# Fewer and wider small products in a decoder kernel: scores by masked keys, queries and scaled keys in one product, and half of a solve's last product

## What is computed

```python
# block 1, delta rule, 4 heads of 32: q and k have length 1
pred = einsum('bhk,bhkv->bhv', k_t, S); err = (v_t - pred) * b_t
S = S + einsum('bhk,bhv->bhkv', k_t, err); o_t = einsum('bhk,bhkv->bhv', q_t, S)
# block 2, attention over ctx, 16 heads of 8, causal
scores = einsum('bhqd,bhkd->bhqk', qh, kh) / sqrt(8); attn = softmax(causal(scores))
# block 4, self attention, 16 heads of 8, q and k of length 1
scores = clip(einsum('bhqd,bhkd->bhqk', q, k) * 0.25, -5, 5); softmax(causal(scores) / 1.5)
# block 5, gated attention over ctx, 8 heads of 16
C = einsum('bhid,bhjd->bhij', qh, kh) * exp(Dtilde - max_d) / 4
```

## Time and profile before

| | |
|---|---|
| median of three runs | 4670.56 us |
| profiled execution, its own time | 4663.74 us |
| its span | 4662.0 us |
| TensorE busy | 4477.5 us, 96% of the span |
| VectorE, ScalarE, GpSimd busy | 3554.0, 3497.4, 2654.2 us |
| instructions of TensorE | 66736 matmuls and as many loads |
| chain of waits that ended last | PE 91%, DVE 4%, ACT 3% |

### The profile page before, as it was taken

One profiled execution on the slowest core, in us unless ns is written; L12 is line 12 of the kernel. 1 busy time (PEld: TensorE's weight loads), 2 busy tenths in 40 slices (PEclk: granted clock), 3 DMA queues, 4 the chain that ended last, 5 costly groups with the idle time before them and its releaser, 6 DMA issues.

```text
span 4662.0 us, 160117 instructions
## 1 busy us (share of the span) xinstructions
PE 4477.5 (96%) x66736; PEld 3503.7 (75%) x66736; DVE 3554.0 (76%) x11069; ACT 3497.4 (75%) x9695; POOL 2654.2 (57%) x2212
## 2 busy tenths in 40 slices
PE   7999989999999999999999999999999879999999
PEld 5777767777777777777777777777777668888888
DVE  4555568988888888888888888888888546776675
ACT  3444458888888888888888888888888547776676
POOL 3344357777667666667766667766677423333332
PEclk8777779999999999999999999999999869999999
DMA  3000000000000000000000000000000100000000
GB/s 97 4 4 4 4 2 2 2 2 2 25 2 2 2 2 25 2 2 2 25 2 2 2 25 2 2 2 2 9 6 6 44 1 4 4 4 4 4 4 6
DMA packets 40236, 40.83 MB, mean 9 GB/s; under 512 B 4164, under 2 KB 37976, under 8 KB 38744
## 3 DMA queue, kind: packets, MB, share of 16 engines
q1 hardware_dynamic: 39512, 30.59, 2.2%
HBM read 28.48 MB, written 2.10 MB: 7 GB/s over the span
## 4 chain that ended last, share of the span: by engine, by line
PE 91%; DVE 4%; ACT 3%; issue 1%; POOL 1%; SPq 0%; DMA 0%; ACTq 0%; DVEq 0%; POOLq 0%
PE ps L532 75%; PE ps L536 16%; ACT BIG L883 2%; DVE BIG L1085 1%; ACT L883 1%; DVE sm L1096 1%; DVE BIG L1093 1%; DVE BIG L1090 0%; POOL BIG L1521 0%; DVE sm L1093 0%; ACT BIG L875 0%; POOL sm L1524 0%; DVE sm L1085 0%; DVE BIG L1163 0%; DVE sm L1191 0%
## 5 line engine op out<-in xcount | busy, mean ns | idle before, releaser
L875 ACT ACTIVATE BIG<-ps 128x512 f32<-128x512 f32 (+6 forms) x3216 | 1481.6, 505 | 665.7 <-PE ps L536 471.1
L532 PE MATMUL ps<-WB,BIG 128*128 128x128 f32 (+1 forms) x8576 | 1897.6, 364 | 7.1 <-DVE BIG L1085 5.1
L1521 POOL TENSOR_TENSOR BIG<-BIG,sm 128x1024 f32<-128x1024 f32 (+1 forms) x864 | 1223.4, 1425 | 778.5 <-DVE sm L1093 502.9
L532 PEld LDWEIGHTS ps<-WB,BIG 128*128 128x128 f32 x8576 | 1153.0, 192 | 410.1 <-issue 378.9
L532 PEld LDWEIGHTS ps<-BIG 64*64 64x64 f32 (+2 forms) x43008 | 1002.1, 133 | 285.1 <-issue 205.8
L1521 POOL TENSOR_TENSOR BIG<-BIG 128x512 f32<-128x512 f32 x768 | 974.3, 1277 | 324.5 <-DVE BIG L1085 323.7
L532 PE MATMUL ps<-BIG 64*64 64x64 f32 (+2 forms) x43008 | 1089.2, 222 | 36.2 <-issue 21.5
L1096 DVE TENSOR_REDUCE sm<-BIG 128x8 f32<-128x512 f32 (+3 forms) x1472 | 871.9, 616 | 150.1 <-ACT BIG L883 143.2
L536 PE MATMUL ps<-t_ident,BIG 128*128 128x128 f32 x6016 | 885.2, 284 | 91.4 <-DVE BIG L1093 40.1
L536 PEld LDWEIGHTS ps<-t_ident,BIG 128*128 128x128 f32 x6016 | 715.1, 146 | 249.1 <-issue 106.8
L883 ACT ACTIVATE BIG<-ps,sm 128x64 f32<-128x64 f32 (+1 forms) x3104 | 678.5, 330 | 103.3 <-DVE sm L1096 100.7
(11 more groups left out here) (122 smaller groups left out, 3084.5 us busy)
## 6 DMA issues: line engine op xcount, KB each, us to landing
WB<-in_Wqkv SPq DMA_DIRECT2D x6, 1536.0 KB, 7.0
y_sb<-in_ctx SPq DMA_DIRECT2D x16, 256.0 KB, 3.1
WB<-in_Wo SPq DMA_DIRECT2D x6, 512.0 KB, 8.5
x_sb<-in_x SPq DMA_DIRECT2D x8, 256.0 KB, 4.5
WB<-in_F_W SPq DMA_DIRECT2D x1, 2048.0 KB, 8.7
WB<-in_F_W SPq DMA_DIRECT2D x8, 256.0 KB, 6.3
out<-x_sb SPq DMA_DIRECT2D x8, 256.0 KB, 2.3
WB<-in_W SPq DMA_DIRECT2D x6, 341.0 KB
```

Source lines behind the costliest of these rows:

```text
L532: return te.matmul(o, l, r, start=start, stop=stop, skip_group_check=not check)
L875: return se.activation(o, i, ACT.Copy)
L1521: return pe_.tensor_tensor(o, a, b, op)
```

## The change

The score products swap roles: the plain queries (`qT`, 64 columns of one sequence) are the stationary operand, and the masked keys are the moving one (`k4`, `k2`). The masked copies of one sequence for all four (two) heads of a group are read in one product with a stride, so 8 products of 256 (128) columns stand where there were 32 (16) of 64. In `G` and `D` queries and beta keys lie side by side in `TT`, and one product per head moves both through the keys (128 columns); a second one of 32x32 writes the diagonal block of the second half. `V` covers only the 8 blocks that are not zero, `U` subtracts in place in `Z` in two instructions of 32 partitions, and the zeroed buffer goes.

```diff
@@ TensorE, phases T, G, D
                     for i in range(3):
-                        o = tr(K[:, 128 * i:128 * i + 128], b.QKB[:, 128 * i:128 * i + 128])
+                        c = 128 * (0, 2, 1)[i]
+                        o = tr(K[:, c:c + 128], b.QKB[:, 128 * i:128 * i + 128])
...
-                    for i in range(4):
-                        for h in range(4):
-                            r, q = slice(32 * h, 32 * h + 32), 64 * ((h + half) % 2)
-                            c = 128 * (h % 2)
-                            qT, kT, bT = (b.TT[r, 128 * j:128 * j + 128] for j in range(3))
-                            if i == 0:
-                                o = mm(K2[h // 2][q:q + 64, c:c + 64], kT[:, q:q + 64], qT[:, q:q + 64])
-                            elif i == 3:
-                                o = mm(K2[h // 2][q:q + 32, c + 96:c + 128], kT[:, q:q + 32], bT[:, q + 32:q + 64])
-                            else:
-                                s = slice(q + 32 * i - 32, q + 32 * i)
-                                o = mm(K2[h // 2][s, c + 64:c + 96], kT[:, s], bT[:, s])
+                    qb, kT = b.TT[:, 0:256].rearrange("p (j c) -> p j c", j=2), b.TT[:, 256:384]
+                    at = [(K2[h // 2], slice(32 * h, 32 * h + 32), 64 * ((h + half) % 2), 128 * (h % 2)) for h in range(4)]
+
+                    for k, r, q, c in at:
+                        mm(k[q:q + 64, c:c + 128].rearrange("p (j c) -> p j c", j=2), kT[r, q:q + 64], qb[r, :, q:q + 64])
+                    for k, r, q, c in at:
+                        o = mm(k[q + 32:q + 64, c + 64:c + 96], kT[r, q + 32:q + 64], qb[r, 1, q + 32:q + 64])
@@ TensorE, phase V
-                    o = blocks16(K, b.E, b.W)
+                    for h in range(4):
+                        c = slice(32 * h, 32 * h + 32)
+                        for r in (slice(32, 64), slice(96, 128)):
+                            o = mm(K[r, c], b.E[r, c], b.W[r, c])
@@ TensorE, scores (s and G in DE likewise call it with qT and k4, xc and k2)
-                    o = scores(u.bank[ph], b.q4, b.kT, 512)
+                    o = scores(u.bank[ph], b.qT, b.k4, 512)
...
-            def scores(k, q, kT, n):
-
-                for c in range(0, n, 64):
+            def scores(k, qT, km, n):
+
+                def half(a, bb):
+                    return a[:, 0:n].rearrange("p (i b c) -> p i b c", b=2, c=64)[:, :, bb, :]
+
+                for bb in range(2):
                     for g in range(4):
                         r, par = slice(32 * g, 32 * g + 32), 64 * (g % 2)
-                        o = mm(bank[k + g // 2][par:par + 64, c:c + 64], q[r, c:c + 64], kT[r, c % 128:c % 128 + 64])
+                        o = mm(half(bank[k + g // 2][par:par + 64, :], bb), qT[r, 64 * bb:64 * bb + 64], half(km[r, :], bb))
@@ ScalarE, phase q of AB (T and xc in DE likewise)
-                    copy(b.kT, K[:, 128:256])
+                    copy(b.qT, K[:, 0:128])
                     for i in range(4):
-                        o = act(b.q4[:, 128 * i:128 * i + 128], K[:, 0:128], ACT.Copy, scale=T["hm8"][:, i:i + 1])
+                        o = act(b.k4[:, 128 * i:128 * i + 128], K[:, 128:256], ACT.Copy, scale=T["hm8"][:, i:i + 1])
@@ VectorE, phase U
-                    o = tt(b.U, b.Z, K[:, 0:128], ALU.subtract)
+                    for r in (slice(32, 64), slice(96, 128)):
+                        o = tt(b.Z[r, :], b.Z[r, :], K[r, 0:128], ALU.subtract)
```

More of the change, by code:

```diff
@@ L323, in ab_bufs @@
             b.TT, b.QM, b.AT, b.CX, b.BT = one[:, 1024:1408], one[:, 1408:1664], one[:, 1664:1792], one[:, 1792:1920], one[:, 1920:2432]
-            b.E, b.D, b.X, b.Z, b.W, b.U = (one[:, 2432 + 128 * i:2560 + 128 * i] for i in range(6))
+            b.E, b.D, b.X, b.Z, b.W = (one[:, 2432 + 128 * i:2560 + 128 * i] for i in range(5))
             b.ON, b.oT = b.xnA, b.xA
             b.xnB, b.xc, b.On, b.OT = two[:, 0:128], two[:, 128:384], two[:, 3456:3584], two[:, 3584:3712]
-            b.q4, b.kT = two[:, 384:896], two[:, 896:1024]
+            b.k4, b.qT = two[:, 384:896], two[:, 896:1024]
             b.P, b.PT = ([two[:, 1408 + 1024 * n + 512 * i:1920 + 1024 * n + 512 * i] for i in range(2)] for n in range(2))
@@ L362, in de_bufs @@
             b.xn1, b.xT1, b.qk, b.sq, b.qn = one[:, 0:128], one[:, 128:256], one[:, 256:512], one[:, 512:768], one[:, 768:1024]
-            b.q4, b.kT, b.On, b.oT = one[:, 1024:1536], one[:, 1536:1664], one[:, 3712:3840], one[:, 3840:3968]
+            b.k4, b.qT, b.On, b.oT = one[:, 1024:1536], one[:, 1536:1664], one[:, 3712:3840], one[:, 3840:3968]
             b.P, b.PT = ([one[:, 1664 + 1024 * n + 512 * i:2176 + 1024 * n + 512 * i] for i in range(2)] for n in range(2))
-            b.xn2, b.xc, b.q2 = two[:, 0:128], two[:, 128:384], two[:, 384:640]
+            b.xn2, b.xc, b.k2 = two[:, 0:128], two[:, 128:384], two[:, 384:640]
             b.GB, b.Dm, b.C, b.CT = (two[:, 640 + 512 * i:1152 + 512 * i] for i in range(4))
@@ L606, in pe_ab @@
                         for q in (slice(0, 64), slice(64, 128)):
-                            o = mm(K[q, c], b.QM[q, 64 * h:64 * h + 64], b.U[q, c])
+                            o = mm(K[q, c], b.QM[q, 64 * h:64 * h + 64], b.Z[q, c])
                 elif ph == "o":
@@ L815, in pe_de @@
                     w.wait_ge(*u.on("act", "xc"))
-                    o = scores(u.bank[ph], b.q2, b.xc[:, 128:256], 256)
+                    o = scores(u.bank[ph], b.xc[:, 0:128], b.k2, 256)
                 elif ph == "om":
@@ L912, in act_ab @@
                 elif ph == "W":
-                    w.wait_ge("const", 2)
                     for q in (slice(32, 64), slice(96, 128)):
@@ L1036, in act_de @@
                     for i in range(2):
-                        o = act(b.q2[:, 128 * i:128 * i + 128], K[:, 0:128], ACT.Copy, scale=T["hm16"][:, i:i + 1])
+                        o = act(b.k2[:, 128 * i:128 * i + 128], K[:, 128:256], ACT.Copy, scale=T["hm16"][:, i:i + 1])
                 elif ph == "vc":
@@ L1528, in _ @@
             for p in range(4):
-                pe_.memset(BIG[:, 3200 * p + 2944:3200 * p + 3072], 0.0)
                 o = pe_.memset(V9[p][:, :], 1.0)
```

## The result

| | before | after |
|---|---|---|
| median (four runs each) | 4669.23 us | **4598.52 us** (4590.02 to 4602.38) |
| ratio | | 0.985, interval 0.983 to 0.988 |
| first 128x512 product of stage C starts at | 631.1 us | 567.6 us |
| stage DE, first product with `t_D_W` to TensorE's last matmul | 943.7 us | 944.9 us |
| TensorE at 1.2 GHz ahead of stage C | 313 us | 171 us |

What follows compares the result with a forecast made beforehand. TensorE, busy 96% of the span, was taken as the bound. The terms -18 (issue), +6.4 (G, D), -0.6 (V, s) and -1.5 (DE) made -13.7 us: 4656.9 us against 4670.56, range 4626 to 4682.

Steps and rivals of the forecast that it cites:

- Rival 3: Stage AB: less idle time lifts TensorE's clock, all 16 slow turns become fast, -35 us more, 4622 us; chance 0.12.
- Issue, -18: Stage AB: of 20.7 us in which TensorE waits for instructions, 18 go with fewer instructions; bounds 0 and 21.
- The clock, 0: Stage AB: the sum held no term for a changed clock; mean granted clock expected to stay within 0.70 to 0.80.
- G and D, +6.4: Stage AB, `G` and `D` products: longer streams cost 0.10 us a half at the low clock, 64 halves, +6.4 us.
- V and s, -0.6: AB, `V` and scores: 0.21 us a tile saved, all but 0.02 lost to `O` waiting for `U`; 32 tiles, -0.6 us.
- DE, -1.5: Stage DE, run of score products: 0.10 us a tile less, -3 us, about half waited away behind VectorE, leaving -1.5 us.
- 1: Stage AB: each matmul with its load costs 34 ns, so fewer instructions give -103 us, 4567 us; chance 0.04.
- 2: Stage AB: the idle time moves elsewhere instead of going, about +4 us, about 4672 us; chance 0.18.
- 4: Stage AB: the clock moves down, 16 turns 2.2 us slower each, +35 us, 4692 us; chance 0.08.
- 5: Scores and `G`, AB and DE: long streams do not share the array four at a time, +70 us, 4727 us; chance 0.04.

Runs made afterwards that it cites:

- e7: The changed kernel with its new score roles, but the score products again in 32 (16) products of 64 columns: 4656.38 us, ratio 0.997.
- e5: The changed kernel with TensorE made to pause ahead of `a2`, behind `O`, in 13 tiles, every other one: 4631.08 us, ratio 0.989.
- e6: The changed kernel with 13 pauses of TensorE, in every other tile, between `D` and the transposes `p1`: 4626.22 us, ratio 0.989.
- e11: The changed kernel with 25 pauses of TensorE between `D` and the transposes `p1`, in each tile from 4 to 28: 4641.86 us, ratio 0.993.
- e10: The changed kernel with `V` one place earlier, `U` ahead of `d1` and `b1`, and `G` and `D` as before: 4605.64 us, ratio 0.986.
- e1: The kernel before with only the score products as changed, in AB and DE: 4622.97 us, ratio 0.990.
- e2: The kernel before with only `T`, `G` and `D` as changed: 4669.97 us, ratio 1.000.
- e8: The changed kernel with `V` one place earlier on TensorE and `U` ahead of `d1` and `b1` on VectorE: 4592.63 us, ratio 0.982.

## Why the prediction was wrong

**The step that failed** is the sum's silent assumption that the clock of AB stays where it is. It let 0.92 us of idle time count 0.92 us. Rival 3 named the mechanism and was given 0.12 and 35 us, where 313 us ahead of stage C lay at the low clock. What the runs showed in its place: the low clock fell by 142 us with the idle time, and that is worth 48 to 57 of the 63.5 us that stage AB gained.

*Issue, -18: right.* 19.3 us became 1.5, and fewer instructions are the reason (e7 has 12.0 us with the old count of score products and the new roles; all these waits end 1.2 to 1.6 us behind a packet of instructions).

*The clock, 0: wrong.* e5 and e6 show it without any other edit: 10 us of idle time cost 27 to 28. The earlier trace rows compare two turns that both hold a low stretch, 2.2 us apart, and count the turns of the slow kind; but every turn of the steady loop before held one. The same trace prices it well if all turns are laid side by side. The 27 turns from 70 to 561 us, length against low clock, lie near a straight line: 14.6 us at none and 0.40 us for each us of low clock (0.37 where idle time is a second variable, which then counts 0.97). Two neighbours among them, with 1.7 and 10.2 us of low clock, read:

```profile
435.60:450.70 15.10, 14.73 (x573) 11.71 (x573) 9.70 (x37) 7.09 (x26) 7.12 (x7) 0.95 0.02 4
450.70:469.90 19.20, 17.88 (x574) 14.54 (x573) 9.80 (x37) 8.19 (x30) 7.16 (x7) 0.73 0.02 5
```

The pair of turns after gives 16.63 - 13.99 = 2.64 us for 6.8 us of low clock, 0.39 us each. e6 and e11 less their pauses give only (26.9 - 10.5) / 65 = 0.25 and (51.2 - 20.1) / 99 = 0.31, because a pause also takes the place of other waits (all the idle time of the same 27 turns grew by about 7 us for 10.5 us of pauses, and by 16 for 20.1); the line through their turns, with idle time as a second variable, gives 0.36 and 0.34. For 142.6 us less low clock, 0.34 to 0.40 make 48 to 57 us. How much low clock would go with the idle time, no row of the kernel before tells.

*G and D, +6.4: right in size.* `G`, `b3` and `D` are the 64 matmuls of these rows (their forms are merged), with the transposes behind them, at the low clock and at full:

```profile
315.11 2.28 PE L532 MATMUL ps<-BIG 32*64 32x128 f32 x64
317.33 0.47 PE L536 MATMUL ps<-t_ident,BIG 128*128 128x128 f32 x1
...
239.52 1.50 PE L532 MATMUL ps<-BIG 32*64 32x128 f32 x64
240.96 0.65 PE L536 MATMUL ps<-t_ident,BIG 128*128 128x128 f32 x4
```

2.22 and 1.44 us. By median a half is 0.634 + 0.261 = 0.895 us at the low clock (0.788 before, 0.10 forecast as the cost) and 0.572 at full clock (0.530). 34 halves of 64 start low, where the forecast took all for low: 34 x 0.107 + 30 x 0.042 = +5 us. The sign for the kernel was wrong all the same, since e10 shows that they pay through the clock.

*V and s, -0.6: wrong in size, +4.8.* The scores came out as forecast (1.02 us in e1). But `V` saves 0.04 us, not the 0.14 drawn from half of its 0.29; why half of the products cost nearly as much as all was not tried. And `O` loses 1.28 - 1.02 = 0.26 us to its wait, 0.19 of it idle behind the modelled end of the scores:

```profile
171.83 0.28 DVE L1086 TENSOR_TENSOR BIG<-BIG,ps 128x128 f32<-128x128 f32 x1
...
172.25 0.59 DVE L1086 TENSOR_TENSOR BIG<-BIG,ps 32x128 f32<-32x128 f32 x2
```

```profile
172.90 0.60 PE L532 MATMUL ps<-BIG 64*64 64x32 f32 x14 [0.19 <-DVE BIG L1086]
```

The two `U` take 0.59 us together, as forecast (0.55), but the first starts 0.42 us behind `d1` (172.25 - 171.83) where the one of before started 0.31 behind it (308.85 - 308.54); why was not tried. From the end of the second `U` to `O` lie 0.06 us, where 0.04 was taken. `O` starts 1.28 us behind the scores' start in the median of the turns, where 1.09 stood before: +0.19 a tile, less `V`'s 0.04.

*DE, -1.5: right, and too small to see.* `G2 s1` now takes 3856.62 - 3855.16 = 1.46 us, as forecast, and the wait behind it takes some of it (36.7 us here, 34.6 before, over 863 and 862 us):

```profile
PE ps L536 <- DVE BIG L1094: 36.7, 29, 3.1
...
3855.16 1.53 PE L532 MATMUL ps<-BIG 32*64 32x128 f32 x32
3856.62 0.71 PE L532 MATMUL ps<-BIG,WB 128*128 128x128 f32 x4
```

*Together* by measured terms: -17.8 (issue) + 4.8 (`V`, `s`) + 5 (`G`, `D`) - 48 to 57 (clock) = -56 to -65 for AB, where -63.5 were measured. So the sum closes. That idle time lowers the clock is shown by e5, e6 and e11, where nothing else changed. That its amount is not the whole cause is shown by e1, e10 and e11; what else is (the place of the idle time, the length of the streams) stays open.

*The rivals.* 1 (a price for each instruction, 4567) falls with e2: 1024 matmuls fewer in AB, no gain. 2 (idle time only moves; its own terms add to 4675 and not 4672) is what e1 shows in part, 15.4 us in other places, but not the whole change. 4 and 5 did not happen: 16 matmuls of 256 columns take 1.02 us, so they share the array as those of 64 do.

The Trainium skill, "TensorE: Matmul & The Clock Gate", Part 1, tells of another kernel in which TensorE idles for moments between groups of matmuls often enough that the clock goes up and down. Here the trace agrees: the longest issue wait before was 1.4 us, and 29 of them with 19.3 us went along with a low stretch in every turn. By it rival 3 deserved more weight.

## What to carry to other kernels

Where a stage's granted clock is below 1 and TensorE stands still for short moments in it, an idle microsecond can cost more than one (2.5 to 2.8 here), so price its removal with the clock. Sum the time at the low clock first: it bounds what is at stake (here an estimate of 313 x 0.40 = 125 us). What a microsecond of it costs is in the profile before, if all turns of the loop are compared by length and by low clock, and not two of them. How much of it would go is not in the rows; a few pauses put in on purpose, or taken out, measure it. Merging small products at equal columns pays where instructions are issued faster than they arrive, which shows in waits that end at a fixed distance behind a packet of the instruction queue; and merging products at the cost of columns can pay too.

## What the runs showed that was not expected

- A pause of 0.8 us in every other turn, 10.5 us in all, costs 27 us; 20.1 us cost 51.
- Every issue wait ends 1.2 to 1.6 us behind the landing of a packet of instructions.
- Of two kernels with equal issue waits (e8, e10) the one with 1024 matmuls fewer and more columns had 149 us of low clock, the other 178.
- VectorE takes 0.59 us for two instructions on 32 partitions, the second starting 0.29 behind the first, where one on 128 takes 0.28: a quarter of the partitions costs no less.
- In `V`, 16 matmuls of 32x32 in place of 32 save 0.04 us of 0.68 for `b1` and `V`.
